# Keys and values of the second cross block, projected in an earlier stage and finished on GpSimd

## The chip, the cores and the metric

The kernel runs on one core of one Trainium2 chip. The metric is the device time of one execution in microseconds, the median of several runs. Beside the times there is one profiled execution, from which all rows below come.

## The reference, cut to what matters

Two transformer layers over 4 x 512 tokens of width 512 and a context of the same length and width 256, all in fp32. Layer 0 is a state-space mixer, a cross attention and a sparse top-2 mixture of 8 experts; layer 1 is a channel attention, a second cross attention and a mixture of 12 experts. The change concerns the second cross attention. Its last 16 context tokens of a batch are treated apart, with weights, biases and affine of their own:

```python
y_dca, y_main = y[:, -16:, :], y[:, :-16, :]
kv_dca = (y_dca @ Wkv_dca + bkv_dca).reshape(b, 16, 2, H, HD)
q = _ln((x @ Wq + bq).reshape(b, s1, H, HD), qn_w, qn_b)
kv = concat([y_main @ Wk + bk, y_main @ Wv + bv])      # per head: HD of k, HD of v
k, v = _ln(kv[..., :HD], kn_w, kn_b), kv[..., HD:]     # k_dca likewise with kn_dca_*
ctx = attn(q, k, v) + attn(q, k_dca, v_dca)            # two softmaxes
x = x + ctx @ Wo + bo
```

Here H is 16 heads and HD is 32; `_ln` subtracts the mean of a head's 32 values and divides by the root of their variance plus 1e-6. Keys and values depend on the context alone, not on x.

## The kernel before

The residual `xa` stays in SBUF as 16 tiles of 128 tokens x 512. The stages follow each other in program order, each one a `section`: five engine programs (PE the tensor engine, ACT the scalar engine, the vector engine, GpSimd, and SP, which issues DMAs) with their own order, tied by semaphores, and a barrier of all engines at its end. Ahead of each block stands `norm_all` (L93): statistics on the vector engine, scaling on ACT, transposes on PE, and on SP the loads of the block's weights, which the section waits for.

`experts0` (L1514) handles the first mixture. Routing: top-2 on the vector engine, a count by matmul (`cum`, L1623), lists by matmul (`lst`, L1627) from 0/1 matrices (`low`, L1708). Then 39 tiles of 128 rows: GpSimd gathers rows by index (L1604), PE transposes them and multiplies by the expert's matrix that ACT copies (L1648, L1661), the vector engine evicts, SP stores to `expert_rows` (L1577). Last comes the combine: GpSimd gathers 32 tiles from there (L1615) and the vector engine adds them to `xa` (L1742).

`attn1` (L1750) handles two batches at a time in seven rounds of matmuls (L1778) with eight PSUM banks; GpSimd and SP have no program in it. `cross1` (L1907) loads 7 MB beside its norm and calls `qkv1` (L1941) and `heads1` (L2097). In `qkv1` the vector engine first centres the weights and biases of key and query over each head (subtracting the mean from the weights makes the projected mean zero, L2051 to L2053), and GpSimd splits the last context tile of each batch into a main and a special part (`cl`, L2035 to L2040) and adds the output bias to `xa` (L2043). Then for each batch in turn PE projects k, q and v, four tiles of 128 tokens each (L1980), the vector engine adds the bias while evicting (L2072), ACT squares (L2009), the vector engine sums, takes the root by four steps of Newton and scales (L2078 to L2081), PE transposes (L1990), and ACT applies the affine on the way to `kT` and `xT` (L2017 to L2022). The raw keys lie in the last quarter of `v`. A tile is a product over KC = 2 chunks of context channels, or HC = 4 chunks for q; the last context tile takes two times KC. An fp32 matmul shows as two PE instructions in the profile.

## Time and profile before

| | us |
|---|---|
| median of 3 runs | 3856.45 |
| lowest and highest | 3853.66, 3860.16 |
| the profiled execution | 3849.94 |
| its span | 3848.2 |
| PE busy in it | 3296.1 (86%) |
| vector engine busy | 2539.0 (66%) |
| ACT busy | 1754.5 (46%) |
| GpSimd busy | 1072.2 (28%) |

The span is what the profiler saw between the first and the last instruction. Busy shares are averages over stages with different limits, so the rows of single stretches say more. Where an engine idles, the rows name what ended the idle time, as the engine and the line that it waited for. The tensor engine's clock is given as the share of its full 2.4 GHz that was granted; 0.50 is its lower level of 1.2 GHz.

### The profile page before, as it was taken

What the parts mean: (1) busy time and instruction counts of PE and PEld (TensorE: products, weight loads), DVE (VectorE), ACT (ScalarE), POOL (GpSimd) and SP (SyncE); (2) the same over time, 40 slices, a digit from 0 to 9 for tenths busy, and PEclk for the clock granted to TensorE, in tenths of its full rate; (3) what the DMA queues carried; (4) which work ended last, traced back from release to release, by engine and by line L of the source; (5) the groups of instructions that cost most, each with busy time, mean ns of one, the idle gap of its engine ahead of it and who ended that gap; (6) DMA issues with size and microseconds to landing.
All of it is one profiled execution on the core that took longest, in us unless ns stands there. A gap on an engine that the chain in (4) does not pass through costs nothing. (4 is left out here: it accounts for less than half of the span.)

```text
span 3848.2 us, 38078 instructions
## 1 busy us (share of the span) xinstructions
PE 3296.1 (86%) x12741; PEld 1716.7 (45%) x12741; DVE 2539.0 (66%) x4790; ACT 1754.5 (46%) x3290; POOL 1072.2 (28%) x697
## 2 busy tenths in 40 slices
PE   2751499999999799999999998792999699999964
PEld 2330244444444455455554555441444345655552
DVE  7778899999998555555555555434111768877654
ACT  3657566666665343333433334241101227767521
POOL 0343699999996010101000000123000200000014
PEclk9875799999999899999999998796999899999967
DMA  6114435353532222222111211244000200000046
GB/s 211 68 57 133 162 98 145 99 145 94 136 99 97 71 63 66 77 72 72 58 55 52 63 50 61 80 128 137 0 0 0 82 0 1 1 1 1 1 138 217
DMA packets 180499, 297.65 MB, mean 77 GB/s; under 512 B 23761, under 2 KB 74321, under 8 KB 176977
## 3 DMA queue, kind: packets, MB, share of 16 engines
q1 hardware_dynamic: 167232, 261.48, 21.2%
q0 software_dynamic: 12208, 33.57, 3.3%
q8 instruction: 102, 1.67, 0.2%
q14 instruction: 93, 0.75, 0.1%
q10 hardware_dynamic: 864, 0.18, 0.0%
HBM read 198.55 MB, written 96.60 MB: 77 GB/s over the span
## 5 line engine op out<-in xcount | busy, mean ns | idle before, releaser
L1201 POOL TENSOR_TENSOR sc_dBu<-sc_dtu,xa 128x1024 f32<-128x1024 f32 x256 | 540.0, 2131 | 38.2 <-DMA sc_dtu<-scan_dtu 29.0
L1111 PE MATMUL y_ps<-sc_g,ident 128*128 128x512 f32 x1024 | 476.2, 600 | 18.6 <-POOL sc_g L1189 12.1
L1225 DVE TENSOR_TENSOR_SCAN sc_dA<-sc_dA,sc_dBu 128x1024 f32<-128x1024 f32 x160 | 365.1, 2282 | 6.4 <-POOL sc_dBu L1201 6.4
L1451 ACT ACTIVATE c_p<-c_ps,c_sm 128x512 f32<-128x512 f32 x256 | 195.6, 774 | 352.6 <-DVE c_sm L1492 352.6
L1165 ACT ACTIVATE sc_dA<-sc_dt,a_neg 128x511 f32<-128x511 f32 x512 | 329.6, 676 | 11.1 <-DVE sc_g L1225 9.8
L1491 DVE TENSOR_REDUCE c_sm<-c_ps 128x4 f32<-128x2048 f32 x64 | 146.7, 2292 | 275.2 <-PE c_ps L1414 275.2
L1111 PEld LDWEIGHTS y_ps<-sc_g,ident 128*128 128x128 f32 x1024 | 189.8, 190 | 256.6 <-issue 168.1
L1484 DVE SCALAR_TENSOR_TENSOR xa<-c_ps,c_sm,xa 128x512 f32<-128x512 f32 x256 | 192.1, 751 | 147.1 <-PE c_ps L1405 133.5
L1405 PE MATMUL c_ps<-c_wo,c_oT 128*128 128x512 f32 x512 | 246.5, 605 | 2.3 <-DVE xa L1484 1.6
L1386 PE MATMUL c_ps<-c_xT,c_wq 128*128 128x512 f32 x512 | 232.3, 597 | 5.2 <-DMA c_wq<-in_c_wq_dram 5.2
L1433 PE MATMUL c_ps<-c_pT,c_v 128*128 128x512 f32 x512 | 232.0, 596 | 2.1 <-DVE c_pT L1503 2.1
L1414 PE MATMUL c_ps<-c_kT,c_qT 128*128 128x512 f32 x512 | 230.2, 592 | 0.0
L1225 DVE TENSOR_TENSOR_SCAN sc_g<-sc_dA,sc_dBu 128x1024 f32<-128x1024 f32 x96 | 218.8, 2280 | 0.0
L1189 POOL TENSOR_TENSOR sc_g<-sc_g,xa 128x1024 f32<-128x1024 f32 x96 | 204.4, 2130 | 42.8 <-DVE sc_g L1225 42.6
L1235 DVE TENSOR_TENSOR sc_g<-sc_dA,xa 128x1024 f32<-128x1024 f32 x160 | 196.0, 1225 | 16.3
L2203 ACT ACTIVATE h_p<-h_ps,h_sm 128x496 f32<-128x496 f32 x256 | 170.0, 672 | 80.3 <-DVE h_sm L2232 80.3
L1372 POOL TENSOR_TENSOR e_d<-e_raw,e_wT 128x256 f32<-128x256 f32 x64 | 53.9, 878 | 543.8 <-DMA e_raw<-sparse_table 543.8
L2339 POOL IOTA e_it<- 128x192 f32 x1 | 0.4, 364 | 654.4 <-POOLq L38 654.4
L1584 POOL IOTA e_it<- 128x128 f32 x1 | 0.4, 353 | 603.8 <-POOLq L38 603.8
L1458 ACT ACTIVATE c_pT<-c_ps 128x512 f32<-128x512 f32 x192 | 107.7, 595 | 117.0 <-PE c_ps L1423 117.0
L2139 PE MATMUL h_ps<-c_kT,c_xT 32*128 32x512 f32 x512 | 145.7, 652 | 14.0 <-ACT h_p L2205 11.7
L1386 PEld LDWEIGHTS c_ps<-c_xT,c_wq 128*128 128x128 f32 x512 | 98.0, 192 | 128.7 <-issue 123.3
(490 smaller groups left out, 6306.7 us busy)
## 6 DMA issues: line engine op xcount, KB each, us to landing
kv_w<-in_c_wkv_dram SPq DMA_DIRECT2D x32, 512.0 KB, 4.1
cross_keys<-kv_out SPq DMA_DIRECT2D x64, 256.0 KB, 2.0
cross_values<-kv_out SPq DMA_DIRECT2D x128, 128.0 KB, 1.9
c_kT<-cross_keys SPq DMA_DIRECT2D x64, 256.0 KB, 2.7
c_rk<-cross_rk SPq DMA_DIRECT2D x64, 256.0 KB, 3.3
c_v<-cross_values SPq DMA_DIRECT2D x64, 256.0 KB, 2.7
expert_rows<-e_yt SPq DMA_DIRECT2D x63, 256.0 KB, 2.0
xa<-scan_bc SPq DMA_DIRECT2D x48, 256.0 KB, 7.9
```

What stands on the lines that cost most here:

```text
L1111: ins = pe.matmul(yps[:, k % 2, :], ident[:], g[:, c % GS, n, :], start=False, stop=(m == NCH - 1 and n == NG - 1))
L1165: ins = act.activation(dA[:, c % 2, n, 1:S], dt[:, k % DT, 1:S], ACT.Exp, scale=a_neg[:, k % CT, at:at + 1])
L1189: pool.tensor_tensor(g[:, c % GS], g[:, c % GS], bc[:, NS + m * NG:NS + (m + 1) * NG, :], ALU.mult).then_inc(s_gp, 1)
L1201: pool.tensor_tensor(dBu[:, c % 3], spread(dtu[:, k % DT, :], NG), bc[:, m * NG:(m + 1) * NG, :], ALU.mult).then_inc(s_dBu, 1)
L1225: dve.tensor_tensor_scan(to.rearrange("p n s -> p (n s)"), dA[:, c % 2].rearrange("p n s -> p (n s)"), dBu[:, c % 3].rearrange("p n s -> p ...
L1235: dve.tensor_tensor(g[:, c % GS], dA[:, c % 2], bc[:, NS + m * NG:NS + (m + 1) * NG, :], ALU.mult).then_inc(s_g, 1)
L1386: ins = pe.matmul(ps[:, QB, :], wq[:, h % 2, c, :], xT[:, c, b * S:(b + 1) * S], start=(c == 0), stop=(c == HC - 1))
L1405: pe.matmul(ps[:, YB + j % 2, :], oT[:, j * P:(j + 1) * P], wo[:, h % 2, :], start=True, stop=True).then_inc(s_y, 1)
L1414: ins = pe.matmul(ps[:, SB + j, :], qT[:, j * P:(j + 1) * P], kT[:, n % 2, :], start=True, stop=True)
L1433: ins = pe.matmul(ps[:, OB, :], v[:, n % 2, kt, :], pT[:, kt, :], start=(kt == 0), stop=(kt == TT - 1))
L1451: ins = act.activation(pr[:, j, :], ps[:, SB + j, :], ACT.Exp, scale=rq[:, j:j + 1], bias=bias[:, j:j + 1], accum_out=l[:, j:j + 1])
L1484: dve.scalar_tensor_tensor(out=xt, in0=ps[:, YB + j % 2, :], scalar=rl[:, j:j + 1], in1=xt, op0=ALU.mult, op1=ALU.add).then_inc(s_ye, 1)
```

## The change

Keys and values leave `qkv1`. Each of the 16 context tiles gives two half-products (keys, values), 32 in all, now computed in `experts0` in order n = 0 to 31: 2 before the count, 4 before the lists, 2 before the first expert tile, 24 behind the last one. PE writes them to four of the section's PSUM banks, ACT copies them into three buffers, and SP stores them raw to HBM (`raw_kv`). The context is loaded by batch, two in the norm ahead, two later on. The split last tile comes laid out from the host (`c1_cl`).

In `attn1` SP brings each raw tile back, GpSimd adds the biases to keys and values, takes each head's mean by five halving additions, subtracts it, squares, and sums the squares in the same way into `kst`; SP stores keys and values (`kn`, `vn`). The vector engine takes the root of all 256 sums a partition once, before the last two batches' outputs. The bias loads move to this stage's norm.

`qkv1` then projects only q. Keys are loaded with two buffers (`kr`), scaled by the root on the vector engine and transposed; values are loaded by one DMA at the end. q has two buffers and a buffer of its own for squares. The centring of key weights and biases is gone.

```diff
@@ -1511,7 +1511,15 @@
 XR, YR, GR = 4, 3, 8
 
 
-def experts0(nc, A, d, rows, parts, xa, ident, held):
+NH1, HD, DCA = 16, 32, 16
+MAIN = S - DCA
+HG = P // HD
+LAST = MAIN - (TT - 1) * P
+HALVES = 2 * NB * TT
+EARLY = (2, 6, 8)
...
-            norm_all(nc, "e0", xa, xT, ident, rows=rows, gate=(gw, A["e0_gwT"].rearrange("(c p) e -> p c e", p=P), lps))
+            norm_all(nc, "e0", xa, xT, ident, rows=rows, gate=(gw, A["e0_gwT"].rearrange("(c p) e -> p c e", p=P), lps),
+                     loads=[(wkv[:], A["c1_wkv"])] + context(0) + context(1))
+        stage = sb("k1_out", [P, 3, H])
...
+        banks = (xps[:, 0].rearrange("p c t -> p (c t)"), xps[:, 1].rearrange("p c t -> p (c t)"), yps[:, 1, :], yps[:, 0, :])
...
+                def stored(n):
+                    sp.wait_ge(s_kev, n + 1)
+                    sp.dma_start(raw_kv[n // 2, n % 2], stage[:, n % 3, :]).then_inc(s_kst[n % 3], 16)
+
+                def following(b):
+                    sp.wait_ge(s_kmm, 2 * TT * (b - 1))
+                    for to, src in context(b):
+                        sp.dma_start(to, src).then_inc(s_c[b % 2], 16)
+
+                for n in range(EARLY[-1]):
+                    stored(n)
+                following(2)
                 for i in range(TL):
                     sp.wait_ge(s_ye, i + 1)
                     sp.dma_start(parts[i * P:(i + 1) * P, :], yt[:, i % YR, :]).then_inc(s_st[i % YR], 16)
+                for n in range(EARLY[-1], HALVES):
+                    stored(n)
+                    if n + 1 == 4 * TT:
+                        following(3)
                 for q in range(YR):
                     sp.wait_ge(s_st[q], 16 * len(range(q, TL, YR)))
+                for q in range(3):
+                    sp.wait_ge(s_kst[q], 16 * len(range(q, HALVES, 3)))
...
+                def product(n):
+                    i, (b, j) = n % 2, divmod(n // 2, TT)
+                    if b >= 2 and n % (2 * TT) == 0:
+                        pe.wait_ge(s_c[b % 2], 32)
+                    if n >= 4:
+                        pe.wait_ge(s_kev, n - 3)
+                    if j < TT - 1:
+                        pairs = [(cT[:, b % 2, c, j * P:(j + 1) * P], wkv[:, i, c, :]) for c in range(KC)]
+                    else:
+                        pairs = [(cl[:, b % 2, m, c, :], wkv[:, 2 * m + i, c, :]) for m in range(2) for c in range(KC)]
+                    for k, (lhs, rhs) in enumerate(pairs):
+                        ins = pe.matmul(banks[n % 4], lhs, rhs, start=(k == 0), stop=(k == len(pairs) - 1))
+                    ins.then_inc(s_kmm, 1)
+
+                for n in range(EARLY[0]):
+                    product(n)
                 pe.wait_ge(s_it, 1)
                 pe.wait_ge(s_M, 1)
                 pe.matmul(cum[:, 0, :], ones[:], M[:].rearrange("p a e -> p (a e)"), start=True, stop=True)
                 pe.matmul(cum[:, 1, :], tri[:], M[:].rearrange("p a e -> p (a e)"), start=True, stop=True).then_inc(s_cum, 1)
+                for n in range(EARLY[0], EARLY[1]):
+                    product(n)
                 for a in range(NA):
                     pe.wait_ge(s_low, a * 4 // NA + 1)
                     ins = pe.matmul(lst[:].rearrange("p k i -> p (k i)"), low[:, a, :],
                                     high[:, a].rearrange("p k i -> p (k i)"), start=(a == 0), stop=(a == NA - 1))
                 ins.then_inc(s_lst, 1)
+                for n in range(EARLY[1], EARLY[2]):
+                    product(n)
+                pe.wait_ge(s_kev, EARLY[2])
...
+                for n in range(EARLY[2], HALVES):
+                    if n == EARLY[2] + 2:
+                        pe.wait_ge(s_ye, TL)
+                    product(n)
 
             @block.scalar
             def _(act):
+                def taken(n):
+                    act.wait_ge(s_kmm, n + 1)
+                    if n >= 3:
+                        act.wait_ge(s_kst[n % 3], 16 * (n // 3))
+                    act.activation(stage[:, n % 3, :], banks[n % 4], ACT.Copy).then_inc(s_kev, 1)
+
+                for n in range(EARLY[0]):
+                    taken(n)
                 act.wait_ge(s_df, 1)
                 act.activation(rw[:, 1, :], rw[:, 0, :], ACT.Exp).then_inc(s_e2, 1)
+                for n in range(EARLY[0], EARLY[2]):
+                    taken(n)
                 act.wait_ge(s_tei, 1)
...
+                for n in range(EARLY[2], HALVES):
+                    taken(n)
...
+        bk = sb("k1_bk", [P, 2, H])
+        bv = sb("k1_bv", [P, 2, H])
+        loads = [(w[n][:], A[f"a1_{n}"].rearrange("(c p) n -> p c n", p=P)) for n in ("wq", "wk", "wvT", "wo")]
+        for dst, main, second in ((bk, "c1_bk", "c1_bkd"), (bv, "c1_bv", "c1_bvd")):
+            loads += [(dst[:, 0, :], A[main].partition_broadcast(P)),
+                      (dst[0:LAST, 1, :], A[main].partition_broadcast(LAST)),
+                      (dst[LAST:P, 1, :], A[second].partition_broadcast(DCA))]
+        norm_all(nc, "a1", xa, xT, ident, keep=xn, loads=loads)
...
+            @block.sync
+            def _(sp):
+                def load(t):
+                    q = t % 3
+                    if t >= 3:
+                        sp.wait_ge(s_ks[q], 16 * (t // 3))
+                        sp.wait_ge(s_vs[q], 16 * (t // 3))
+                    sp.dma_start(kb[:, q, :], raw_kv[t, 0]).then_inc(s_kl[q], 16)
+                    sp.dma_start(vb[:, q, :], raw_kv[t, 1]).then_inc(s_vl[q], 16)
+
+                for t in range(2):
+                    load(t)
+                for t in range(NB * TT):
+                    if t + 2 < NB * TT:
+                        load(t + 2)
+                    q = t % 3
+                    sp.wait_ge(s_vd, t + 1)
+                    sp.dma_start(vn[t], vb[:, q, :]).then_inc(s_vs[q], 16)
+                    sp.wait_ge(s_kd, t + 1)
+                    sp.dma_start(kn[t], kb[:, q, :]).then_inc(s_ks[q], 16)
+                for q in range(3):
+                    sp.wait_ge(s_ks[q], 16 * len(range(q, NB * TT, 3)))
+                    sp.wait_ge(s_vs[q], 16 * len(range(q, NB * TT, 3)))
+
+            @block.gpsimd
+            def _(pool):
+                own = Order(pool, s_kown)
+                parts = ksq[:].rearrange("p (h d) -> p h d", d=HD)
+
+                def summed(x, to):
+                    n = HD // 2
+                    while n:
+                        out = parts[:, :, 0:n] if n > 1 else to
+                        own.after(pool.tensor_tensor(out, x[:, :, 0:n], x[:, :, n:2 * n], ALU.add))
+                        x, n = parts, n // 2
+
+                for t in range(NB * TT):
+                    q, part = t % 3, t % TT // (TT - 1)
+                    heads = kb[:, q, :].rearrange("p (h d) -> p h d", d=HD)
+                    pool.wait_ge(s_vl[q], 16 * (t // 3 + 1))
+                    pool.tensor_tensor(vb[:, q, :], vb[:, q, :], bv[:, part, :], ALU.add).then_inc(s_vd, 1)
+                    pool.wait_ge(s_kl[q], 16 * (t // 3 + 1))
+                    own.after(pool.tensor_tensor(kb[:, q, :], kb[:, q, :], bk[:, part, :], ALU.add))
+                    summed(heads, mean[:].unsqueeze(2))
+                    own.after(pool.tensor_scalar(mean[:], mean[:], 1.0 / HD, None, ALU.mult))
+                    own.after(pool.tensor_tensor(heads, heads, along(mean[:], HD), ALU.subtract))
+                    pool.tensor_tensor(ksq[:], kb[:, q, :], kb[:, q, :], ALU.mult).then_inc(s_kd, 1)
+                    pool.wait_ge(s_kd, t + 1)
+                    summed(parts, kst[:, 0, t * NH1:(t + 1) * NH1].unsqueeze(2))
+                pool.sem_inc(s_ss, 1)
...
+                    if b0 + 2 == NB:
+                        dve.wait_ge(s_ss, 1)
+                        own.after(dve.tensor_scalar(kst[:, 0, :], kst[:, 0, :], 1.0 / HD, 1e-6, ALU.mult, ALU.add))
+                        rsqrt(dve, own, kst[:, 1, :], kst[:, 0, :], kst[:, 2, :])
...
+            kr = sb("c1_kr", [P, 2, TT, H], c=c2)
+            norm_all(nc, "c1", xa, xT, ident, loads=[
+                (wq[:], A["c1_wq"].rearrange("(c p) n -> p c n", p=P)),
+                (bq[:], A["c1_bq"].partition_broadcast(P)),
+                (kr[:, 0], kn[0:TT].rearrange("t p n -> p t n")),
+                (kr[:, 1], kn[TT:2 * TT].rearrange("t p n -> p t n")),
+                (bo[:], A["c1_bo"].partition_broadcast(P)), (aff[:], A["c1_aff"])])
+            qkv1(nc, A, wq, bq, bo, wo, aff, xT, kr, kn, vn, kst, kT, v, xa, ident, c2)
...
+    TURNS = [("k", 0), ("k", 1), ("q", 0), ("k", 2), ("q", 1), ("k", 3), ("q", 2), ("q", 3)]
...
+            sp.dma_start(wo[:], A["c1_wo"].rearrange("(c p) n -> p c n", p=P)).then_inc(s_v, 16)
+            for b in range(2, NB):
+                sp.wait_ge(s_T, (TURNS.index(("k", b - 2)) + 1) * HC)
+                sp.dma_start(kr[:, b % 2], kn[b * TT:(b + 1) * TT].rearrange("t p n -> p t n")).then_inc(s_kl[b % 2], 16)
+            sp.dma_start(v[:].rearrange("p b j n -> p (b j) n"), vn.rearrange("t p n -> p t n")).then_inc(s_v, 16)
+            sp.wait_ge(s_v, 32)
...
-            project("k", 0)
-            for b in range(NB):
-                project("q", b)
-                turned("k", b)
-                project("v", b)
+            turned("k", 0)
+            project(0)
+            turned("k", 1)
+            for b in range(1, NB):
+                project(b)
+                turned("q", b - 1)
                 if b + 1 < NB:
-                    project("k", b + 1)
-                turned("q", b)
+                    turned("k", b + 1)
+            turned("q", NB - 1)
...
-            squares("k", 0)
-            for b in range(NB):
-                squares("q", b)
-                turned("k", b)
+            turned("k", 0)
+            squares(0)
+            turned("k", 1)
+            for b in range(1, NB):
+                turned("q", b - 1)
                 if b + 1 < NB:
-                    squares("k", b + 1)
-                turned("q", b)
+                    turned("k", b + 1)
+                squares(b)
+            turned("q", NB - 1)
...
-            pool.memset(cl[:, :, 0, :, LAST:P], 0.0)
-            pool.memset(cl[:, :, 1, :, 0:LAST], 0.0)
-            for b in range(NB):
-                end = (b + 1) * S
-                pool.tensor_copy(cl[:, b, 0, :, 0:LAST], cT[:, :, end - P:end - DCA])
-                ins = pool.tensor_copy(cl[:, b, 1, :, LAST:P], cT[:, :, end - DCA:end])
-            ins.then_inc(s_cl, 1)
...
+            def keyed(b):
+                if b >= 2:
+                    dve.wait_ge(s_kl[b % 2], 16)
+                x = kr[:, b % 2].rearrange("p j (h d) -> p (j h) d", d=HD)
+                r = kst[:, 1, b * TT * NH1:(b + 1) * TT * NH1]
+                dve.tensor_tensor(x, x, along(r, HD), ALU.mult).then_inc(s_kn, 1)
...
-            centre(bk[:].rearrange("p a n -> p (a n)"), 2 * NH1)
-            centre(wkv[:, 0].rearrange("p c n -> p (c n)"), KC * NH1)
-            centre(wkv[:, 2].rearrange("p c n -> p (c n)"), KC * NH1, s_wk)
-            centre(bq[:], NH1)
-            centre(wq[:].rearrange("p c n -> p (c n)"), HC * NH1, s_wq)
+
+            keyed(0)
+            own.after(centre(bq[:], NH1))
+            centre(wq[:].rearrange("p c n -> p (c n)"), HC * NH1).then_inc(s_wq, 1)
+            keyed(1)
             for b in range(NB):
-                taken("k", b)
-                normalise("k", b)
-                taken("q", b)
-                normalise("q", b)
-                taken("v", b)
+                taken(b)
+                normalise(b)
+                if b + 2 < NB:
+                    keyed(b + 2)
```

## Rows read from the trace of the kernel before

**Rows 1.** The page's first line: span and instructions of the one core.

```profile
span 3848.2 us, 38078 instructions
```

**Rows 2.** Table of stretches: start:end, length, busy us by engine, clock, DMA share, GB/s.

```profile
2385.00:2422.00 37.00, 36.60 (x192) 36.39 (x192) 13.11 (x40) 14.99 (x24) 0.00 (x0) 0.55 0.30 114
2422.00:2448.00 26.00, 4.91 (x37) 3.26 (x36) 19.46 (x86) 2.99 (x3) 4.25 (x13) 0.50 0.04 11
2448.00:2602.00 154.00, 153.32 (x467) 75.77 (x468) 49.73 (x77) 71.61 (x38) 34.51 (x37) 0.98 0.42 130
2606.00:2654.00 48.00, 0.00 (x0) 0.00 (x0) 23.95 (x32) 0.00 (x0) 35.14 (x32) 0.52 0.63 175
2683.00:2997.00 314.00, 312.53 (x792) 146.00 (x792) 57.90 (x113) 29.00 (x64) 0.00 (x0) 1.00 0.00 0
3007.00:3025.00 18.00, 10.85 (x64) 7.94 (x64) 13.93 (x41) 15.24 (x24) 0.50 (x2) 0.90 0.83 279
3037.00:3185.00 148.00, 140.75 (x416) 68.49 (x415) 103.13 (x190) 40.66 (x56) 15.40 (x11) 0.99 0.00 1
```

**Rows 3.** Timeline (start, length, engine, line) from routing into the first expert tiles.

```profile
2427.56 1.19 PE L1623 MATMUL e_cum<-e_M,e_ones 128*128 128x256 f32 x2 [5.50 <-DVE e_M L1678]
...
2438.38 4.63 DVE L1708 TENSOR_TENSOR e_low<-e_slot_f,e_dst 128x1024 bf16<-128x1024 f32 x4
...
2445.23 3.71 ACT L1661 ACTIVATE e_de<-e_d 128x2048 f32 x2 [17.47 <-DVE e_tei L1713]
...
2450.70 5.31 PE L1648 MATMUL e_yps<-e_de,e_xsT 128*128 128x512 f32 x8
...
2460.16 3.60 PE L1648 MATMUL e_yps<-e_de,e_xsT 128*128 128x512 f32 x8
```

**Rows 4.** Timeline of the combine's first gather, last addition, and the next norm's start.

```profile
2606.21 0.94 POOL L1615 DMA_INDIRECT e_gy<-expert_rows,e_row  x1 [24.62 <-DMA expert_rows<-e_yt]
...
2653.35 0.75 DVE L1742 SCALAR_TENSOR_TENSOR xa<-e_gy,e_rw,xa 128x512 f32<-128x512 f32 x1 [0.70 <-DMA e_gy<-expert_rows,e_row]
...
2657.46 4.84 DVE L143 BATCH_NORM_STATS2 st_a<-xa 128x6 f32<-128x512 f32 x8 [3.35 <-PEq L38]
```

**Rows 5.** DMA issues: target and source, queue, count, KB each, median us to landing.

```profile
expert_rows<-e_yt SPq DMA_DIRECT2D x39, 256.0 KB, 2.0
```

**Rows 6.** Groups of instructions, stretch 3024 to 3190: busy us, mean ns, idle before.

```profile
L1980 PE MATMUL q_ps<-c_wkv,c_cT 128*128 128x512 f32 x96 | 45.2, 623 | 18.2 <-DVE c_wkv L2053 13.5 <-DVE c_v L2072 4.7
L1980 PE MATMUL q_ps<-c_wkv,c_cl 128*128 128x512 f32 x64 | 28.8, 592 | 0.0
```

**Rows 7.** Timeline of the second cross block's projections, their start and end.

```profile
3028.31 24.09 POOL L2043 TENSOR_TENSOR xa<-xa,c_bo 128x512 f32<-128x512 f32 x16
...
3036.57 7.71 PE L1980 MATMUL q_ps<-c_wkv,c_cT 128*128 128x512 f32 x12 [13.54 <-DVE c_wkv L2053]
...
3043.07 3.28 DVE L2053 TENSOR_TENSOR c_wq<-c_wq,q_mw 128x2048 f32<-128x2048 f32 x1
...
3169.99 1.91 PE L1990 MATMUL q_ps<-ident,c_v 128*128 128x128 f32 x16
...
3170.92 1.91 ACT L2009 ACTIVATE c_wq<-q_raw 128x2048 f32<-128x2048 f32 x1 [10.89 <-DVE q_raw L2072]
...
3172.86 2.29 DVE L2078 TENSOR_REDUCE q_st<-c_wq 128x64 f32<-128x2048 f32 x1 [1.98 <-ACT c_wq L2009]
...
3178.98 2.29 DVE L2081 TENSOR_TENSOR q_raw<-q_raw,q_st 128x2048 f32<-128x2048 f32 x1
...
3182.03 2.78 ACT L2017 ACTIVATE c_xT<-q_ps,c_aff 128x512 f32<-128x512 f32 x4 [5.56 <-PE q_ps L1990]
...
3185.57 1.14 PE L2139 MATMUL h_ps<-c_kT,c_xT 32*128 32x512 f32 x8 [2.27 <-PEq L38]
```

**Rows 8.** GpSimd: bias additions (min/median/max ns), and the smallest addition (busy us, mean ns).

```profile
L2043 POOL TENSOR_TENSOR xa<-xa,c_bo x16: 1253/1262/3317, 3028.3 to 3051.1; 128x512 f32<-128x512 f32 x16
...
L518 POOL TENSOR_TENSOR new<-old,tot 128x8 f32<-128x8 f32 x32 | 17.3, 542 | 70.9 <-DMA old<-sparse_table,locu 63.7 <-issue 7.3
```

156 lines of the change are left out of this document (66 added, 90 removed).

## The prediction

> **What bounds the kernel now.** I read the profile in this order: the page's span, the table of stretches, the timelines at the seams of the stages, and last the groups of instructions. The change touches four of the stages, which follow each other with a barrier between any two, so a stage's own critical chain decides what an edit in it is worth. The span is 3848.2 us [rows 1], and the execution around it took 3849.94 us; the median of the three runs is 3856.45 us, 6.5 us more. The sum below is made against the profiled execution and then carried to the median as a difference.
>
> The table of stretches [rows 2] shows three kinds of stage. From 2422 to 2448 (routing of the first experts) PE is busy 4.9 of 26 us, and the vector engine sets the pace. From 2448 to 2602 (the 39 expert tiles) PE is busy 153.3 of 154 us. From 2606 to 2654 (the combine) PE and ACT do nothing at all and the DMA engines are 0.63 busy. The first attention, 2683 to 2997, has PE busy 312.5 of 314 us, and GpSimd idle. The projections of the second cross block, 3037 to 3185, have PE busy 140.8 of 148 us: this is the stage that the change empties.
>
> **Taken out of the cross block.** Keys and values cost 96 instructions on the whole tiles and 64 on the split last tiles [rows 6]. An instruction is half of one fp32 matmul. The rows' mean of 592 to 623 ns overlaps its neighbour; the spacing is read from eight instructions in 3.60 us and their last one's overhang [rows 3], that is 0.43 us each. 160 x 0.43 = 68.8 us of PE. Before it, PE also waited for the vector engine to centre the key weights, until 3036.57 [rows 7].
>
> What is left there is not PE alone, so I lay the new order out in time. The section begins at about 3024.5. Vector: scaling of the ready keys of batch 0, 128x2048, 2.29 us alone as in [rows 7], 3.28 us if GpSimd's bias additions run beside it (the centring of c_wq, same size, shows 3.28) [rows 7]; I take 3.3. The centring of bq and wq took from 3036.55 to 3046.35, 9.8 us, and is unchanged. So PE may begin the query projection at 3037.6. A batch is 32 instructions x 0.43 = 13.7 us; the first pays some 2.1 us for the lower clock, as twelve instructions took 7.71 us at this place and not 5.3 [rows 7]. Query batch 0 ends at 3053.5, keys of batch 1 are turned (16 transposes, 1.9 us [rows 7]), query batch 1 ends at 3069.0. From there a batch costs its 13.7 us plus some 4 us, because turning q and then k through the same four banks waits on ACT (four evictions take 2.78 us [rows 7]): ends at 3086.7 and 3104.2. Beside it runs the chain of a batch: take four tiles, square 1.91, reduce 2.29, the square root's small steps to 3178.98, scale 2.29 [rows 7], 8.4 us from the square's end to the scaled queries, 16.5 us in all with the two turnings that ACT does before the square. It just fits under a batch. After the last query batch nothing hides it: taking to 3106.7, ACT's q evictions first, square to 3109.4, normalising to 3117.8, turning and eviction to 3121.3, barrier, heads at about 3122.2. Before they began at 3185.57 [rows 7]. Gain 63.4 us. Bounds: 68.8 if the chain were wholly hidden; 50 if each of three batches waited another 4 to 5 us for its neighbour.
>
> Loads: the keys of two batches (2 MB), wq, and small ones replace 7 MB ahead of the projections; the old load was over before the stage ended, so nothing is gained. The values (4 MB) and wo load while queries are projected. At the 279 GB/s of [rows 2] that takes 18 us of a stage of 97.
>
> **Put into the first expert stage, before its loop.** The eight half-products of batch 0 are 2 + 4 + 2. Two run while the vector engine finds the top experts: eight instructions that start at the lower clock (granted 0.50, which is 1.2 GHz, in this stretch [rows 2]), 5.3 us as in the first tile [rows 3], so from 2422.9 to 2428.2 or a little later, against a count matmul that started at 2427.56. That one then runs at the higher clock and makes up for it: 0 to +2 us. Four run until the lists are ready (first slice at 2439.6 [rows 3]): 4 x 1.72 = 6.9 us at the higher clock, 13.8 us at the lower, room of 10 us: nothing, or +4. Two last ones, both of the split tile, come after the lists at 2443.8: 16 instructions, 6.9 us, to 2450.7, and PE then waits for their copies. ACT copies the last one before it copies the first expert's matrix, which it began at 2445.23 [rows 3] and now begins near 2451.4. First expert product at 2453.5 in place of 2450.70; it needs 3.6 us and not the 5.31 that it took from a cold start [rows 3]. Net +1.3 us (0 to +5.5). PE sets the loop itself, which has no new work: 0.
>
> In the norm ahead, 3.5 MB of loads go before the row stores on SP's queue. DMA is 0.30 busy in those 37 us [rows 2] and PE, at the 0.55 clock, is 36.6 us busy: hidden.
>
> **Put behind the loop.** 24 half-products, 96 + 64 less the first 40 instructions, 120 x 0.43 = 51.6 us on an idle PE, from 2602.6. Then a copy, about 0.6 us (an estimate from ACT's 1.91 for four times as many columns [rows 7]), and the last store; a 256 KB store lands 2.0 us after its issue [rows 5]. End near 2657.3, next norm about 0.9 us later at 2658.2, plus the shift of 1.3. The combine ended at 2653.35 + 0.75, and the norm began at 2657.46 [rows 4]. So PE's chain alone is 0.7 us over it, +2.1 with the shift. What is unknown is DMA. The 32 gathers are 0.63 x 48 / 32 = 0.95 us of all engines each; the loop's 0.42 x 154 = 64.7 us for 37 gathers and 37 stores leaves 0.80 us a store. 24 stores add 19 us, the context of the last batch some 2.5 us, to the 30 us of the gathers: 52 us in a stage of about 53. The highest share shown is 0.83 [rows 2], by which the stage would last 63 us, +9. Against that, bytes: 15.5 MB at the 279 GB/s of that same row are 55 us, +2 or so. Three output buffers give a store 5.2 to 6.4 us for its round trip, against 2.0. I take +3 (0 to +10). Sum for this stage 2.1 + 3 = +5.1 us.
>
> **GpSimd in the attention.** Per tile: four full passes (two biases, mean subtraction, squares), two trees of five additions over 256 down to 16 elements, one scaling by 16. A full pass is 1.26 us by the median of the bias additions, 8 elements take 0.54 [rows 8]. A line between these two gives 0.90, 0.71, 0.62, 0.58, 0.55 for the tree, 3.4 us; twice that, 5.05 for the full passes, 0.55, and about 1 us of waits on itself: 13.3 us a tile, 213 us for 16. The vector engine asks for the result only before the last two batches' outputs, some 286 us into the stage. So 17.9 us a tile is free. The fifteen small vector steps there (6 to 7 us) stand before additions whose matmuls take 27 us more: hidden, or 6 us if GpSimd came late. The sixteen round trips of 1 MB on an unused DMA: hidden.
>
> The tall row of the bias additions is 3317 ns against a median of 1262 [rows 8], in a stretch where the vector engine is busy throughout, so the two do hold each other up. All sixteen took 24.1 us there instead of 20.2 [rows 7], a factor of 1.19. The Trainium skill (GPSIMD Engine Reference, section 8, Key points) says that GpSimd shares its SBUF interfaces with VectorE and that they contend when the latter has two SBUF inputs or a two-port mode. The trace agrees with it on these rows. In the attention the vector engine is busy 57.9 of 314 us [rows 2], nearly always reading PSUM, so even 1.19 would leave 254 us, inside 286.
> The skill's section 4.1 (Engine selection) of the same page speaks against the change: two-input elementwise work belongs on VectorE, GpSimd being about twice as slow. The rows agree on the speed, but this kernel has the vector engine on a chain and GpSimd on none.
>
> **Sum.** -63.4 + 5.1 = -58.3; with up to 1 us for barriers that clear more semaphores, -57. 3849.9 - 57 = 3793 for an execution like the profiled one, 3856.45 - 57 = about 3800 for the median.
>
> **Rivals.** (A) As summed, 3792 to 3810: 0.65. (B) The combine becomes a DMA stage: gathers and stores crowd each other to the 0.83 share and more, +9 to +20 over the sum, 3808 to 3820. For: 52 us of transfers in 53. Against: gathers are paced by GpSimd's issue, 1.4 us each, and have eight buffers. 0.15. (C) The cross block's new chain (take, square, reduce, root, scale, with ACT turning two tiles in between) is longer than a batch: +5 to +15, 3805 to 3815. For: by my layout the scaled queries are ready only 0.3 to 0.4 us before PE asks for them. 0.10. (D) Slower: each of GpSimd's 16 steps a tile is held up some 0.7 us by vector instructions, 24 us a tile. 384 us is 98 over the free 286, result -57 + 98 = +41, 3897. It decides from 21.4 us a tile on, (286 + 57) / 16. For: the 3317 ns row. Against: the factor of 1.19 under a full vector engine. 0.04. (E) The change does not do what it says, that is, the PE work moves but what it leaves behind is held by something else (late values or keys, GpSimd at 21 us a tile), within 0.2%: 0.03. Better than 3792: 0.03.
>
> A measurement of this kernel can tell 0.2%, about 8 us, from no change. Faster 0.93, same 0.03, slower 0.04. Range 3790 to 3822, which leaves out (D), (E), and the ends of (B).
>
> **What would show it.** The heads' first matmul should come about 57 us earlier, near 3128, and 97 to 98 us behind its section's start. The attention must still last 314 us with GpSimd busy 190 to 230 of them. First expert tile near 2453 and the norm after the combine at 2660 to 2668, with DMA above 0.8 in the combine. The forecast is wrong if PE has gaps in the attention, if GpSimd's work crosses 286 us, if the combine grows past 65 us, or if PE runs at the lower clock through the query projections (13 us a batch more).

## The result and the profile after

The changed kernel takes 3809.56 us (median of 4 runs, 3798.11 to 3809.9) against 3855.05 us for the kernel before in the same session (4 runs, 3842.35 to 3860.16). The ratio is 0.9887, 95% interval 0.9871 to 0.9903: about 44 us faster, where 57 were forecast, and inside the range of 3790 to 3822. The profiled execution was the shortest of the four, 3798.11 us; the other three lie between 3809.51 and 3809.9. In all that follows, ratios and intervals leave out one execution at a lower clock, 5961.85 us at a mean granted clock of 0.58 in the run with four gather buffers. The page of the profiled execution begins

```profile
span 3796.4 us, 38397 instructions
```

which is 51.8 us under [rows 1]. The same kernel run once more (called "after again" below) was profiled at a span of 3809.7 us. The two traces differ mainly in one place, and that place is most of this study. The next table goes through the program by marks that every trace has, in us; the last two columns are differences from the kernel before, each rounded by itself.

| from, to | before | after | after again | after | after again |
|---|---|---|---|---|---|
| start, norm of the first experts | 2385.4 | 2386.8 | 2385.3 | +1.4 | -0.1 |
| norm, first expert matmul | 65.3 | 67.0 | 69.6 | +1.7 | +4.2 |
| first, last expert matmul | 151.4 | 149.8 | 149.8 | -1.6 | -1.6 |
| last expert matmul, next norm's first turning | 65.0 | 66.1 | 84.2 | +1.2 | +19.3 |
| norm's first turning, last attention matmul | 328.9 | 329.5 | 329.3 | +0.6 | +0.4 |
| last attention matmul, heads' first | 189.6 | 128.6 | 127.8 | -61.0 | -61.8 |
| heads' first, last | 472.1 | 475.0 | 473.3 | +2.8 | +1.2 |
| heads' last, last addition of the second experts | 186.8 | 189.9 | 186.7 | +3.2 | -0.1 |
| sum | | | | -51.8 | -38.5 |

Table of stretches of the kernel after, the profiled execution of the result, with the columns of [rows 2] (busy us by PE, PEld, DVE, ACT, POOL, then clock, DMA share, GB/s). The stretches are the routing, the expert loop, the combine, the attention, and the second cross block's projections.

```profile
2424.00:2450.00 26.00, 21.25 (x72) 10.23 (x72) 16.64 (x50) 4.29 (x8) 3.86 (x4) 0.84 0.30 98
2451.00:2605.00 154.00, 152.36 (x471) 75.25 (x472) 50.32 (x78) 74.81 (x40) 33.07 (x35) 1.00 0.42 132
2606.00:2656.00 50.00, 49.62 (x116) 21.66 (x114) 23.57 (x32) 13.50 (x23) 34.70 (x32) 1.00 0.89 301
2687.00:3000.00 313.00, 312.53 (x792) 146.01 (x792) 66.11 (x127) 28.99 (x64) 140.69 (x240) 1.00 0.15 54
3028.00:3127.00 99.00, 76.29 (x256) 42.02 (x256) 62.25 (x94) 33.45 (x52) 26.22 (x16) 0.87 0.22 75
```

Against [rows 2] the routing's PE went from 4.91 to 21.25 us busy, the combine's from nothing to all of it, and the attention has the same 312.53 us of PE with 140.69 us of GpSimd beside it. The projections last 99 us and not 148. Now the last three of these stretches in "after again":

```profile
2606.00:2656.00 50.00, 35.92 (x75) 14.77 (x74) 23.74 (x32) 8.14 (x14) 32.67 (x32) 0.86 0.77 252
2706.00:3018.00 312.00, 311.73 (x791) 146.01 (x792) 66.03 (x126) 29.00 (x64) 140.67 (x240) 1.00 0.15 54
3046.00:3145.00 99.00, 76.08 (x256) 41.88 (x256) 62.36 (x95) 33.23 (x52) 26.21 (x16) 0.87 0.22 75
```

Of the three only the combine differs. PE did 75 matmul instructions in its 50 us and not 116, and the DMA engines were less busy, 0.77 and not 0.89. The PE timeline of "after again" shows where (start, length, engine, line, operands, idle before):

```profile
2622.24 3.60 PE L1670 MATMUL e_xps<-k_w,k_cT 128*128 128x512 f32 x8
2625.68 3.60 PE L1670 MATMUL e_yps<-k_w,k_cT 128*128 128x512 f32 x8
2630.09 1.98 PE L1670 MATMUL e_xps<-k_w,k_cT 128*128 128x512 f32 x4 [0.81 <-issue]
2637.80 3.67 PE L1670 MATMUL e_xps<-k_w,k_cT 128*128 128x512 f32 x4 [5.73 <-issue]
2647.59 5.61 PE L1670 MATMUL e_yps<-k_w,k_cl 128*128 128x512 f32 x8 [6.12 <-issue]
2654.61 3.70 PE L1670 MATMUL e_yps<-k_w,k_cl 128*128 128x512 f32 x8 [1.41 <-ACT k_out L1721]
```

Products of four instructions that belong 1.72 us apart come 7.7 and 9.8 us apart, until the last gather has landed at about 2653. The next norm pays: its vector engine waits 24.9 us for PE's end of the section, 3.7 us in the trace of the result.

```profile
L143 DVE BATCH_NORM_STATS2 st_a<-xa 128x6 f32<-128x512 f32 x16 | 9.7, 680 | 24.9 <-PEq L38 24.9
```

### The profile page after: what moved, and what is told of

Same layout as the page of the kernel before. It is cut to its first block and busy times, and to the rows that moved or that the text cites. A ratio compares the mean times of both kernels' runs of the same rounds, so it can differ in the third digit from the quotient of the medians.

```text
span 3796.4 us, 38397 instructions
## 1 busy us (share of the span) xinstructions
PE 3303.2 (87%) x12729; PEld 1722.7 (45%) x12741; DVE 2493.5 (66%) x4700; ACT 1766.4 (47%) x3318; POOL 1207.5 (32%) x927
## 5 line engine op out<-in xcount | busy, mean ns | idle before, releaser
L1111 PE MATMUL y_ps<-sc_g,ident 128*128 128x512 f32 x1024 | 476.3, 600 | 18.4 <-POOL sc_g L1189 12.0
L1165 ACT ACTIVATE sc_dA<-sc_dt,a_neg 128x511 f32<-128x511 f32 x512 | 329.5, 676 | 11.0 <-DVE sc_g L1225 9.8
L2249 PE MATMUL h_ps<-c_kT,c_xT 32*128 32x512 f32 x512 | 147.3, 663 | 13.3 <-ACT h_p L2315 11.7
```

Of the source, the lines that this page charges most:

```text
L1111: ins = pe.matmul(yps[:, k % 2, :], ident[:], g[:, c % GS, n, :], start=False, stop=(m == NCH - 1 and n == NG - 1))
L1165: ins = act.activation(dA[:, c % 2, n, 1:S], dt[:, k % DT, 1:S], ACT.Exp, scale=a_neg[:, k % CT, at:at + 1])
```

## The experiments

All ratios are to the kernel before on the same chip; medians of different runs can come from different chips, so small differences between them are read from the ratios or the traces. The question of the first eleven was the missing 13 us of the median and each large term of the sum.

**After again: the changed kernel once more.** No edit.

> The changed kernel once more, unaltered, for a second trace and a tighter interval. Two readings of the gap between the forecast gain (57 us) and the measured ratio (0.9887, about 44 us). Theory 1, phase of TensorE's clock: the cross block still gives 55 to 60 us (from the first norm of the experts to the heads' first matmul) in every trace, and what is missing lies in stages whose code is unchanged, where the stretch at the low clock begins earlier or ends later: up to 3 us each in the heads' first 100 us and in the two norms with gate. Ratio 0.985 to 0.989. Theory 2, the chain behind the query projections or the combine is slower in other executions than in the traced one: then the gain up to the heads' first matmul is under 50 us in this trace.

Measured: 3809.39 us (6 runs, 3799.48 to 3814.84), ratio 0.99 (0.9882 to 0.9918). Its trace is the one above. The cross block's gain (-61.8) is whole, and the combine gives back 19.3.

**Without the 24 products behind the loop.** This kernel leaves them out; batches 1 to 3 of the second cross block take batch 0's raw keys and values.

```diff
-                for n in range(EARLY[2], HALVES):
-                    if n == EARLY[2] + 2:
-                        pe.wait_ge(s_ye, TL)
-                    product(n)
...
-                    sp.dma_start(kb[:, q, :], raw_kv[t, 0]).then_inc(s_kl[q], 16)
+                    sp.dma_start(kb[:, q, :], raw_kv[t % TT, 0]).then_inc(s_kl[q], 16)
```

> The changed kernel without the 24 half-products behind the expert loop, their copies, stores and the third reload; batches 1 to 3 take batch 0's raw keys and values, so that part of the computation is left out. In the trace the combine with them moved 276 GB/s at a DMA share of 0.82 and PE's last product ended at 2655.6, the last addition at 2656.4. If they cost what I reckoned for PE's chain and crowding together (5 us, of which 3 for the DMA), the next norm begins 2.5 to 5 us earlier relative to the first expert tile and the kernel is 3 to 5 us faster than the changed one. If they were free: below 1 us. If crowding reached further (a full DMA stage): 8 us or more.

Measured: 3793.03 us (4 runs, 3785.69 to 3793.99), ratio 0.9855 (0.9835 to 0.9875), span 3792.3. Last expert matmul to the norm 64.6 us against 65.0 before the change. By the ratios (0.99 and 0.9855) what stands behind the loop costs about 17 us of the typical run, and the rest of the change is worth some 56.

**The 24 products computed and copied, but not stored.** This kernel leaves out their stores; the later batches take batch 0's raw data as above.

```diff
-                for n in range(EARLY[-1], HALVES):
-                    stored(n)
-                    if n + 1 == 4 * TT:
-                        following(3)
+                following(3)
```

> The changed kernel with the 24 products behind the loop computed and copied, but not stored (batches 1 to 3 take batch 0's raw keys and values; their stores are left out). It takes the DMA stores away and leaves PE's and ACT's work. If the stores are what costs, PE runs the 24 products in 51.6 us without a gap and the kernel is 12 to 18 us faster than the changed one, nearly as fast as the one without these products (ratio 0.9855 to the kernel before), with 2 us for PE's chain. If PE's or ACT's work itself costs: less than half of that.

Measured: 3792.07 us (4 runs, 3779.27 to 3795.48), ratio 0.9845 (0.9828 to 0.9861). Last expert matmul to the norm 65.0 us, the wait ahead of the norm 3.2 us, DMA share 0.63. Its combine:

```profile
2606.00:2656.00 50.00, 44.17 (x103) 19.19 (x101) 26.41 (x37) 12.11 (x21) 32.19 (x29) 0.96 0.63 181
```

PE is done with the products 51.5 us behind the last expert matmul, as in the trace of the result, against 70.2 in "after again". With gathers and products but no stores, nothing stalls: it takes the stores beside the gathers.

**Eight store buffers in place of three**, in the experts' own matrix buffer, which is free behind the loop.

```diff
-                    sp.dma_start(raw_kv[n // 2, n % 2], stage[:, n % 3, :]).then_inc(s_kst[n % 3], 16)
+                    buf, sem, _ = buffer(n)
+                    sp.dma_start(raw_kv[n // 2, n % 2], buf).then_inc(sem, 16)
```

> The changed kernel with eight buffers in place of three for the 24 half-products behind the expert loop (in the buffer of expert matrices, which is free by then). In the second trace of the changed kernel PE stood still for some 20 us there, because ACT waited 5 to 9 us for a store to land before it could reuse one of three buffers, while GpSimd's gathers ran; the norm that follows began 25 us after the last addition. Theory 1, the stores' time to landing beside the gathers, times three buffers, is the bound: with eight the products end 51 to 55 us after the loop, the next norm begins 3 to 6 us after the last addition, and the kernel gains 10 to 18 us over the changed one (ratio to the kernel before 0.985 or less). Theory 2, the DMA engines' bandwidth is used up: the buffers fill, PE stalls as before or the gathers get slower by as much; gain below 4 us.

Measured: 3807.01 us (4 runs, 3804.46 to 3808.6), ratio 0.9878 (0.9862 to 0.9895), span 3806.9. Last expert matmul to the norm 77.4 us. The interval overlaps that of the changed kernel: eight buffers bring little or nothing, where 10 to 18 us were expected if the ring of three were the bound. A wait on a full ring is not the main cause.

**24 store buffers**, one for each product, so that no copy waits for a store.

```diff
+            def buffer(n):
+                if n < EARLY[-1]:
+                    return stage[:, n % 3, :], s_kst[n % 3]
+                m = n - EARLY[-1]
+                return d[:, m // NE0, m % NE0, :], s_kd
```

> The changed kernel with a buffer for each of the 24 half-products behind the loop (in the expert matrices, free by then), so that neither PE nor ACT ever waits for a store. Eight buffers had left PE standing for some 12 us, as the hardware queue of the stores moved only 4.9 MB in the 50 us in which the gathers moved 8.4. Theory 1, the stores are served slowly only while gathers run and PE's work piles up behind them: here PE ends its products 52 us after the loop, the rest of the stores (some 2 MB) drains in 7 to 10 us once the gathers are done, and from the last expert matmul to the attention's first transposes it takes 70 to 75 us, against 84 in the second trace of the changed kernel, 77 with eight buffers and 65 before; ratio to the kernel before 0.985 to 0.987. Theory 2, the volume of transfers alone sets the end: 77 to 80 us as with eight buffers.

Measured: 3809.46 us (4 runs, 3808.11 to 3809.78), ratio 0.9905 (0.9889 to 0.9922), span 3808.0, last expert matmul to the norm 77.5 us, where 70 to 75 were expected if only full buffers held PE back. Its ACT and PE timelines, the copies first:

```profile
2631.50 0.60 ACT L1732 ACTIVATE e_d<-e_yps 128x512 f32<-128x512 f32 x1 [1.12 <-issue]
2634.63 0.60 ACT L1732 ACTIVATE e_d<-e_yps 128x512 f32<-128x512 f32 x1 [2.53 <-PE e_yps L1679]
2640.26 0.60 ACT L1732 ACTIVATE e_d<-e_xps 128x512 f32<-128x512 f32 x1 [5.03 <-PE e_yps L1679]
2645.20 0.60 ACT L1732 ACTIVATE e_d<-e_xps 128x512 f32<-128x512 f32 x1 [4.35 <-PE e_xps L1679]
2651.63 0.60 ACT L1732 ACTIVATE e_d<-e_yps 128x512 f32<-128x512 f32 x1 [5.83 <-DMA u<-in_in_proj_wT_dram]
2658.01 0.60 ACT L1732 ACTIVATE e_d<-e_yps 128x512 f32<-128x512 f32 x1 [5.79 <-DMA u<-in_in_proj_wT_dram]
2658.51 1.08 ACT L1732 ACTIVATE e_d<-e_xps 128x512 f32<-128x512 f32 x2
```

```profile
2633.01 3.60 PE L1679 MATMUL e_xps<-k_w,k_cT 128*128 128x512 f32 x8
2636.45 7.03 PE L1679 MATMUL e_yps<-k_w,k_cl 128*128 128x512 f32 x16
2643.31 1.88 PE L1679 MATMUL e_xps<-k_w,k_cT 128*128 128x512 f32 x4
2645.85 1.98 PE L1679 MATMUL e_xps<-k_w,k_cT 128*128 128x512 f32 x4 [0.66 <-issue]
2652.28 3.68 PE L1679 MATMUL e_yps<-k_w,k_cT 128*128 128x512 f32 x4 [4.44 <-ACT e_d L1732]
```

PE's line at 2633.01 is products 20 and 21, recorded over by 2636.6. ACT has a free buffer for each and waits for nothing but PE's signal, yet it copies them at 2640.26 and 2645.20 (counted from the first copy), product 23, over by 2643.5, at 2658.01, and the next ones at once when the gathers are through (last addition 2658.9). So neither the ring nor a missing input holds the chain: between the last matmul of a product and the copy that its signal releases lie 5.4 to 14.5 us, where the first copies of this section follow within 0.1. PE follows ACT, since it may be only four banks ahead.

The trace also keeps the times at which semaphores were updated (not all of them), and they say on which side of the signal the time is lost. For this run, in us:

| product | its last matmul, recorded end | its signal recorded | ACT's copy starts |
|---|---|---|---|
| 8 | 2610.86 | 2610.88 | 2610.90 |
| 20 | 2634.89 | 2640.23 | 2640.26 |
| 21 | 2636.61 | 2645.18 | 2645.20 |
| 22 | 2640.04 | 2651.61 | 2651.63 |
| 23 | 2643.48 | 2657.99 | 2658.01 |
| 24 | 2645.19 | 2658.05 | 2658.51 |
| 25 | 2647.84 | 2658.11 | 2658.99 |

ACT starts 0.02 us after the signal, or right behind its previous copy: it is not ACT that is late, it is PE's signal. Nor is it the products: 23, 24 and 25 follow each other on one engine and a product takes 1.72 us or more, while their signals come 0.06 us apart. They had been done and their signals were held. In "after again" the signals of products 16 to 19 come 5.3, 11.3, 19.4 and 24.7 us behind the recorded ends, and the one of product 19 is followed within 0.12 us by two more. The executions divide without exception: in all nine traces with eight gather buffers and the stores some signals are late, by 6.3 us at most in the trace of the result and by 14 to 25 us in the other eight; in the three traces that have the products without the stores or with four or five gather buffers, every recorded signal stands 0.01 to 0.02 us behind its product's end.

**Four gather buffers in place of eight**, three store buffers as in the change.

```diff
 def experts0(nc, A, d, rows, parts, xa, ident, held, raw_kv):
+    GR = 4
```

> The changed kernel with four gather buffers in place of eight in the combine of the first experts, and three store buffers as in the changed kernel. If the stores land late because up to eight gathers of 256 KB stand ahead of them in the DMA engines, four in flight let a store land in half the time: PE's stall behind the loop falls from 20 us to below 8, the combine's last addition comes 0 to 8 us later, gain 5 to 12 us over the changed kernel. If the queue of gathers has nothing to do with it, the stall stays and the kernel is the same or slower by what the gathers lose.

Measured: 3799.33 us (median of all 4; three lie between 3794.78 and 3801.29), ratio 0.9857 (0.9838 to 0.9877), span 3795.6. Its combine:

```profile
2606.00:2656.00 50.00, 50.00 (x118) 22.11 (x117) 17.76 (x24) 13.13 (x22) 25.73 (x26) 1.00 0.79 259
```

PE is never idle in it and the wait ahead of the norm is 3.1 us, but the gathers themselves are slower: the last addition starts 59.2 us behind the last expert matmul (52.0 in the trace of the result, 48.9 in "after again"), the norm 72.7 us. Copies still wait up to 3.8 us for a store, and the lead of four banks hides it. With fewer gathers in flight the stall is gone, with the same bytes.

**GpSimd's additions in the cross block held until the query weights are centred.**

```diff
+            pool.wait_ge(s_wq, 1)
             for t in range(NB * TT):
                 pool.tensor_tensor(xa[:, t, :], xa[:, t, :], bo[:], ALU.add)
```

> The changed kernel with one wait added: GpSimd adds the output bias to the residual only after the query weights are centred. In the changed kernel's trace keys' scaling took 3.39 us, the one of 512 columns 1.71, the scaling of the means 1.26 and the last subtraction 3.28, all beside GpSimd. If the two engines hold each other up, those four fall to about 2.3, 0.7, 0.2 and 2.3 us, the first query matmul comes 4 to 5 us earlier, and the kernel is 4 to 5 us faster. If the slow rows are the operations' own, nothing changes, or it gets slower by the later bias additions.

Measured: 3806.43 us (5 runs, 3800.55 to 3808.75), ratio 0.9892 (0.9874 to 0.9909). By the trace the last attention matmul to the first query matmul falls from 42.0 to 37.4 us: the two engines hold each other up there by 4.6 us, within the 4 to 5 expected. The total can't tell so little.

**Twelve matmuls of constant data ahead of the last turning**, to see what the lower clock behind an idle PE costs.

```diff
+            pe.wait_ge(s_ev, NB * TT)
+            for n in range(12):
+                pe.matmul(ps[:, n % TT, :], wq[:, 0, 0:P], wq[:, 1, :], start=True, stop=True)
             turned("q", NB - 1)
```

> The changed kernel with 12 further matmuls of constant data on PE in the gap behind the last query projection (PE idle 11.8 us there), results unused. If the low clock after that gap is what makes the last transposes take 3.67 us and not 1.9, and the heads' first 100 us run at 0.89 of the clock and not 0.93, those transposes fall to about 1.9 us and the heads' first stretch to 0.93 or more: 3 to 5 us faster in all. If the clock has nothing to do with the gap, no difference.

Measured: 3804.81 us (6 runs, 3791.68 to 3811.43), ratio 0.9888 (0.9868 to 0.9907). The 16 transposes take 1.97 us in place of 3.67, the stretch from the last query matmul to the heads 18.4 in place of 19.4, and the heads' length (471.8) stays within the 471.6 to 475.0 of the other traces of this change. About 1 us, no more, where 3 to 5 were expected.

**GpSimd's mean tree done five times**, which makes its work longer than the attention can hide.

```diff
-                    summed(heads, mean[:].unsqueeze(2))
+                    for _ in range(5):
+                        summed(heads, mean[:].unsqueeze(2))
```

> The changed kernel with the tree of additions for the mean done five times instead of once, same result. GpSimd's work took 9.9 us a tile in the trace (from the first key load's addition at 2691.7 to the last at 2840.3), 160 us in all; a tree of five takes some 2.5 us, so four more make it 20 us a tile and 320 us. By my sum the vector engine needs the result 286 us into the stage and a tile has 17.9 us free: the attention should last 35 to 45 us longer, and the kernel should be 0 to 15 us faster than the one before instead of 40. If GpSimd's time were on the path already, four trees would cost their whole 160 us; if something else hid it, nothing.

Measured: 3818.65 us (4 runs, 3813.56 to 3821.86), ratio 0.9928 (0.9911 to 0.9944), 9.3 us above the changed kernel. GpSimd takes from 2704.5 to 3013.7, 19.3 us a tile. The vector engine's timeline shows the wait that now decides:

```profile
3013.81 0.29 DVE L2038 TENSOR_SCALAR k_st<-k_st 128x256 f32<-128x256 f32 x1 [26.58 <-POOLq L1912]
```

The wait of 26.58 us begins 286.0 us behind the stage's first matmul, where the prediction had put the need at 286. What it costs was forecast wrongly: PE's part of the attention still lasts 312.1 us and not 35 to 45 us longer, and the heads come 10.5 us later behind it than in "after again", so that the kernel is 28 us faster than the one before and not 0 to 15.

**Eight store buffers, and a new order in the cross block:** the query weights centred first, GpSimd behind that, squares ahead of the keys' evictions, the last batch squared and normalised in halves.

```diff
-            for b in range(NB):
+            for b in range(NB - 1):
                 taken(b)
                 normalise(b)
...
+            normalised_halves(NB - 1)
```

> Eight buffers as above, and three changes in the second cross block: the query weights are centred first and projected before the keys are turned; GpSimd's bias additions wait for the centred weights; the squares go ahead of the keys' evictions on ACT, and the last batch is normalised in two halves. Beginning: the first query matmul 8 us earlier (vector engine 4.8 us of centring instead of 13.3), less 2 us for the turnings. End: from PE's last query matmul to the heads' first 12 us and not 19. Sum 10 to 15 us on top of the eight buffers, ratio 0.979 to 0.983 to the kernel before. If the chain over the vector engine, and not its beginning and end, bounds the projections, only 4 to 6 us.

Measured: 3799.08 us (4 runs, 3793.85 to 3805.78), ratio 0.9866 (0.9849 to 0.9882). Last attention matmul to first query matmul 33.6 us (42.0), but to the heads 124.8 (127.8): two turnings of keys in a row behind the first projection cost PE 6.5 us. By the medians that is 8 us under "eight store buffers", where 10 to 15 were expected.

**24 store buffers and that order with one turning of keys behind each projection.**

```diff
-    TURNS = [("k", 0), ("k", 1), ("q", 0), ("k", 2), ("q", 1), ("k", 3), ("q", 2), ("q", 3)]
+    TURNS = [(what, b) for b in range(NB) for what in ("k", "q")]
```

> The same 24 buffers, and the second cross block in a further order: weights centred first, GpSimd's bias additions after them, one turning of keys behind each query projection in place of two behind the first (which made PE wait 6.5 us for ACT's evictions), squares ahead of the keys' evictions, last batch normalised in halves. From the attention's last matmul to the heads' first: 128.6 and 127.8 us in the two traces of the changed kernel, 124.8 in the last kernel. If its two turnings were what cost, 115 to 119 us here, and the kernel is 9 to 13 us faster than with the 24 buffers alone; ratio to the kernel before 0.982 to 0.984. If the chain over the vector engine fills in, 122 to 125 us.

Measured: 3790.71 us (4 runs, 3784.34 to 3795.81), ratio 0.9857 (0.984 to 0.9873). Last attention matmul to the heads is 119.0 us, 8.8 under "after again" and 9.5 under the run with 24 buffers. The medians of these two differ by 18.8 us; most of the rest is in code that is the same in both (routing 4.3 us, second experts' norm 6.7), and no edit explains it. The combine stalls as in the run with 24 buffers (the norm 77.6 us behind the last expert matmul).

**Five gather buffers and the new order**, with the change's three store buffers.

```diff
 def experts0(nc, A, d, rows, parts, xa, ident, held, raw_kv):
+    GR = 5
```

> The changed kernel with two edits that other runs tried apart: five gather buffers in the first expert stage in place of eight, and the new order in the second cross block (query weights centred first, GpSimd's bias additions behind that, one keys' turning behind each query projection, last batch squared and normalised in halves). In the run with 24 store buffers no product had to wait for a store, and still the copies of products 20 to 23 came 5.0 to 6.4 us apart while the gathers ran; with four gathers in flight, or without the stores, they kept 1.72 us. Theory 1 (the number of gathers in flight beside the stores holds up the chain of products): five are near four, the copies keep 1.72 us, and the last addition comes at 2657 to 2664 (GpSimd needs 1.25 us a gather; with four in flight a gather took 1.75 us, so five give about 1.4); last expert matmul to the next norm's first turning 66 to 71 us, against 84.3 in the changed kernel taken again and 72.8 with four. Theory 2 (any queue of gathers deeper than the additions' pace does it, and four was at the edge): the copies spread again, and the stretch is 77 to 85 us. In both, last attention matmul to first head matmul is 119 us (127.8 without the new order, 119.0 with it in the run with 24 buffers). Profiled execution by theory 1 3776 to 3790 and ratio 0.980 to 0.984; by theory 2 3788 to 3798 and 0.984 to 0.988.

Measured: 3783.24 us (5 runs, 3780.29 to 3783.96), ratio 0.9836 (0.9823 to 0.985), span 3778.8: faster than both kernels of the case. Its combine:

```profile
2606.00:2656.00 50.00, 50.00 (x118) 22.05 (x117) 21.90 (x30) 13.73 (x23) 33.65 (x32) 1.00 0.88 290
```

PE is never idle in it, the last addition comes at 2661.2 and the norm 68.4 us behind the last expert matmul, as the first theory wanted. That is 15.9 us less than in "after again", but 2.2 more than in the trace of the result, which did not stall: fewer gathers buy a combine that does not stall, not a shorter one. Last attention matmul to the heads is 118.6 us. The copies did not keep 1.72 us, as that theory also said: one waited 6.58 us for a store and others about 2 us, and the four banks of lead absorbed it. PE's signals were all on time.

## Why the prediction was right, and where it was off

**The removal, -63.4.** Measured -61.0 and -61.8 over the stretch with its norm. The heads' first matmul stands at 3127.77, where the prediction's check said near 3128. That is partly luck: the block gave 2.4 us less than forecast, while the whole first expert stage of this execution cost 1.2 us and not 5.1, and its norm began 1.4 later. The section began at 3027.7, by the same 28.5 us behind the last attention matmul as before; the last query batch ended 81.1 us behind that (79.7 forecast) and the heads followed 19.0 us later (18.0 forecast). The rows of the result are

```profile
3028.44 3.39 DVE L2179 TENSOR_TENSOR c_kr<-c_kr,k_st 128x2048 f32<-128x2048 f32 x1 [0.77 <-PEq L38]
...
3041.73 16.34 PE L2103 MATMUL q_ps<-c_wq,c_xT 128*128 128x512 f32 x32 [6.17 <-DVE c_wq L2172]
...
3108.80 1.91 PE L2114 MATMUL q_ps<-ident,q_raw 128*128 128x128 f32 x16
3122.52 3.67 PE L2114 MATMUL q_ps<-ident,q_raw 128*128 128x128 f32 x16 [11.81 <-DVE q_raw L2194]
```

From the scaling of the keys at 3028.44 to the first query matmul are 13.3 us, where 13.1 were forecast (3.3 + 9.8). Rival C did not come about: between the query batches PE does turnings and nothing else.

**Routing with the loop, +1.3 (0 to +5.5).** The first expert matmul came 1.7 and 4.2 us later behind the norm, and the loop was 1.6 us shorter in both, since its first tile no longer starts cold: 0.0 and +2.6 together. The two last early products took 9.12 us where 6.9 were put, with a granted clock of 0.79 from 2442 to 2451. The 0.0 owes something to chance. Over the thirteen traces with this change norm and routing took 65.1 to 74.6 us (65.3 before), in the order of the clock granted from 2385 to 2422: 65.1 us at 0.66, 67.0 at 0.59 (the trace of the result is one of the two), 69.4 to 69.9 at 0.55, which is also the clock of the trace of before, and 72.4 to 74.6 at 0.50. At the same clock as before the term is +2.6, and at 0.50 it is up to +7.6, beyond its bound of 5.5. The kernel before has one trace, so how far its own stretch moves is not known.

**GpSimd.** A tile took 9.9 us and not 13.3. The mean of a full pass was right for the biases and high for the rest:

```profile
L1904 POOL TENSOR_TENSOR k_kb<-k_kb,k_bk 128x512 f32<-128x512 f32 x16 | 20.4, 1275 | 0.0
L1907 POOL TENSOR_TENSOR k_kb<-k_kb,k_mean 128x512 f32<-128x512 f32 x16 | 16.8, 1047 | 1.3
L1895 POOL TENSOR_TENSOR k_sq<-k_sq 128x32 f32<-128x32 f32 x32 | 7.7, 242 | 2.5
```

The line drawn to the 542 ns row of [rows 8] failed at its low end: additions of 16 to 64 columns cost 214 to 322 ns, so the 542 ns of that row was something of its own. Rival D's slowing did not come: the bias additions in the attention took 1265 ns in the median and 1441 at most, against 1262 and 3317 in [rows 8]. The run with five trees shows that the crossing lies where it was put, and what passing it costs: of a wait of 26.6 us, 10.5 arrive at the heads, because additions and small steps lie behind it that the attention's last matmuls no longer cover.

A rule of the Trainium skill (SBUF — State Buffer, Who interferes with whom) says that a vector instruction with two SBUF inputs contends with a GpSimd instruction that reads SBUF, and one with a single input outside the two-port modes does not. The traces agree on both sides: scaling the keys took 3.39 us beside GpSimd's additions and 2.29 without them, while the copies out of PSUM in the attention kept their 0.69 us, and the reduction of the query weights, with one input, its 2.29 us. Other steps with one full input were slowed, though: 0.53 us and not 0.17 for 16 columns and 1.26 and not 0.20 for 64 in the centring, and in the attention the sixteen scalings of `a_wo`, 652 ns in the mean and not 482 as before. Whether they ran in a two-port mode no trace shows.

**Behind the loop, +5.1, of which 1.3 was the shift from ahead and +3 (0 to +10) was for DMA.** This is the term that was mis-sized: the stretch itself grew by 1.2 in the trace of the result, by 19.3 in the repeated one, and by 17 us by the median of the run without the products. That is rival B's size (+9 to +20 over the sum) but not its reason. The median of 3809.56 lies in rival A's range and in B's alike, so the total alone would not have told them apart. B, and my own term, held that the DMA engines' share would cap near the 0.83 of [rows 2] and stretch the transfers. In fact the share rose to 0.89 in the execution that did not stall, fell to 0.77 in the one that did, and the gathers ended 3 us earlier behind the loop in the one that stalled (last addition 48.9 us behind the last expert matmul, 52.0 in the other). What stretched was PE's chain of products, which I had taken as 51.6 us of work on an idle engine, with the contention priced by bytes alone. The 51.6 us were right where nothing stalled (51.5 measured), and 70.2 where it did. In the sum itself a slip of 0.5 us was made: 2602.6, 51.6, 0.6 and 2.0 give 2656.8 and not 2657.3.

**Shown:** PE's signals come late with stores and eight gather buffers together, not without the stores and not with four or five; ACT starts as soon as they come; they catch up with the end of the gathers. The execution of the result had late signals too, up to 6.3 us, and its four banks of lead covered them, so whether PE stalls is a matter of how late they get. **Not shown:** what in the chip holds the signals, and why one execution gets 6 us and another 25. The engines' own instructions arriving late is an unlikely reason: the 50 us of the combine hold one packet on each of the two instruction queues in both traces, the one with the stall and the one without. Untested are three or six and seven gather buffers, and stores issued from another queue. The same page of the Trainium skill says under its practical consequences that a DMA never contends with a compute engine. No run here speaks against it: copies took their 0.60 us throughout, and the matmuls that took longer (3.67 us for four instructions and not 1.98) ran behind a pause of PE at a granted clock of 0.50. What was late was a signal between two engines, of which that sentence says nothing.

**What the sum did not have.** In the trace of the result the heads took 2.8 us more and the second experts' norm with what follows 3.2 us more, in code that did not change. The clock granted in the first 100 us of the heads was 0.89 against 0.93, and in the norm the time at the lower level was longer (0.55 over the 60 us from 3600 here, 0.56 over the 50 us from 3660 before). In the repeated run the second of these is gone (-0.1). Over all traces of this change that last stretch took 179.3 to 189.9 us, in code that no edit touched, so single traces and small sets of runs carry some 10 us of chance. The best version had 181.6 us there, 5.2 less than before. In its edited stretches it is 15.9 and 9.2 us shorter than the stalled "after again", 25 us in all; by the ratios it is 20 to 25 us ahead of the changed kernel.

## What to carry to other kernels

An idle engine beside a stage of gathers is not free: where a chain of signals (product, copy, store) runs beside gathers and stores, test it with fewer transfers in flight before giving it more buffers. Here five gather buffers took 15.9 us off the stalled combine, 24 store buffers 6.8. Take a second trace before explaining a gap between forecast and median: the first one here was the execution that did not stall. When a copy starts late, compare its start with the time of the signal that it waits for; that told a late signal from a late engine. Moving elementwise work to an idle GpSimd cost nothing while the vector engine read PSUM; find the instruction that waits for it and compare it with the work's length, which decides within a few us.

## What was not expected of the hardware

With eight gathers and stores in flight, signals of PE's finished products were recorded 5 to 15 us late, with a free buffer and a DMA share of 0.78 ("24 store buffers"), then three within 0.12 us of each other; ACT started 0.02 us behind the first. Five gathers in flight beside the same stores moved 290 GB/s at a share of 0.88 without it. GpSimd additions of 16 columns took 0.22 us, far under the 0.54 us of the small one in [rows 8]. A vector step of 16 columns took 0.53 us beside GpSimd's additions and 0.17 us without them.
